# The isomorphism round's inverse deviation: Heron steps on VectorE in place of ScalarE's square root

## The chip, the cores and the metric

The kernel runs on one core of one Trainium2 chip. The metric is the device time of one execution in microseconds. The engines are PE (TensorE), ACT (ScalarE), DVE (VectorE), POOL (GpSimd) and SP (SyncE, which here only issues DMAs). The host only lays the arrays out.

## The reference

Four graph networks run one after the other over the same 50000 nodes of 128 numbers and 25000 edges. Each is followed by a residual sum and a layer norm. The change is in the second network alone, a graph isomorphism layer (GIN):

```python
def _layernorm(x, axis=-1, eps=1e-05):
    m = jnp.mean(x, axis=axis, keepdims=True)
    v = jnp.var(x, axis=axis, keepdims=True)
    return (x - m) / jnp.sqrt(v + eps)
...
        edge_emb = edge_attr @ bond_W + bond_b
...
        message = jax.nn.gelu(x[src] + edge_emb, approximate=False) * edge_weight
        agg = jax.ops.segment_sum(message, dst, num_segments=x.shape[0])
        h = (1.0 + eps) * x + agg
        h = jax.nn.relu(h @ W1 + b1)
        return h @ W2 + b2
...
    x = _layernorm(x + _L1_gnn_ref(x, edge_index, edge_attr_16, edge_weight1, L1_gnn_bond_W, L1_gnn_bond_b, L1_gnn_eps, L1_gnn_W1, L1_gnn_b1, L1_gnn_W2, L1_gnn_b2), axis=-1)
```

So every row of 128 numbers needs its mean and one divided by the root of its variance.

## The kernel before

The work is eight rounds: three of SAGE, one of GIN, two of GCN, two of RGCN. A round goes through the nodes in 49 pairs of halves; a pair is 1024 nodes, 8 blocks of 128 rows. The GIN round is the branch `k == 3` everywhere, and it takes about 1500 to 2400 us of the profile.

Each engine has its own instruction stream, written out by hand, that walks through the same steps `it` of 49 pairs; semaphores hold the streams together. No scheduler reorders anything, so each engine does its work in the order of its step function, and the pipeline between pairs comes from the offsets (`it - 1`, `it + 1`) in those functions. In most steps there is also an edge batch (896 edges, 28 of them in all), which must be ready before the next half can be summed. The order of the work within a GIN step is:

- ACT, if there is a batch: copies the weighed edge messages to half precision (L791) and forms the gelu of the next batch (L785). Then for the pair: `sums_out(it, 1)` (L831), `hidden(it, 0)` (L840), `deviation(it - 1)` (L866, the square root), `sums_out(it + 1, 0)`, four blocks of `normalise(it - 1)` (L881), `hidden(it, 1)`, the other four blocks.
- DVE, if there is a batch: the low part of the messages (L1532) and the next batch's embedding sum (L1504). Then the one-hots that turn edges into sums (L1550), `add(it - 1, 1)` (L1630), `statistics(it - 1, 1)` (L1640, L1645), `scale_rows(it - 2)` (L1757), the one-hots of the next pair's second half, `scale_and_move(it - 1)` (L1654 and L1656: inverse deviation, and minus mean times it), `add(it, 0)`, `statistics(it, 0)`.
- PE, if there is a batch: its embedding (L1075). Then per half the products of messages and one-hots (L1116, L1118), the node's own rows (L1142), the first dense layer (L1180) and the second (L1188, L1192).
- POOL weighs the messages after the gelu (L710) and issues the gathers of later batches (L680). SP loads rows and stores the normalised ones.

ACT holds one table of functions at a time. Copy, Relu and Identity stand in any table; Gelu and Sqrt stand in different ones. Loads of tables (ACT_TABLE_LOAD) are put into the stream by the compiler ahead of the instruction whose line they carry.

`wait_apart` is a wait that is an instruction of its own, followed by an increment of an unused semaphore; `wait` is carried by the instruction behind it:

```python
            eng.wait_ge(semaphore, value)
            eng.sem_inc(passed, 1)
```

Of the kernel before, what the change touches and what calls it, by code (L numbers as in the profile page):

```python
# [7 lines left out]
I32 = mybir.dt.int32  # L8
U16 = mybir.dt.uint16
ALU = mybir.AluOpType  # L10
# [27 lines left out]
GROUPS = -(-TILES // GROUP)  # L38
TURNS = BATCHES // RING
EPS = 1e-5  # L40
assert TILES % BATCH == 0 and BATCHES % RING == 0 and TILES % 2 == 0

SAGE, GIN, GCN, RGCN = "sage", "gin", "gcn", "rgcn"
# [17 lines left out]
class StepSemaphores:  # L61
# [3 lines left out]
    NAMES = ("taken", "high", "low", "every", "out", "feature", "rows", "rows_copied", "turned", "turn_copied", "agg",  # L65
             "bn", "var", "std", "rstd", "moved", "normed", "copied", "turned_edges", "masked_done", "masked_used",
             "hidden_made", "hidden_done", "scaled", "emb_done", "emb_used", "gelu_done", "weighed_edges",
             "gain_step", "gained", "bn2", "var2", "std2", "rstd2", "moved2", "normed2", "sum_made")


    def __init__(self, shared, totals, part, rel):
# [34 lines left out]
        self.weighed = one("weighed_edges", BATCHES + 1, gin)  # L106
        self.res_loaded = pair("residual", 16 * NPAIR, last and part != 4)
        self.bn_done = one("bn", NHALF, last)
        self.var_done = one("var", NPAIR, last)
        self.std_done = one("std", NPAIR, last)  # L110
        self.rstd_done = one("rstd", NPAIR, last)
        self.moved = one("moved", NPAIR, last)
        self.normed = one("normed", NPAIR, last)
# [32 lines left out]
def build_gnn(nc, A, out_ap, rounds=ROUNDS):  # L146
# [3 lines left out]
    with ctx:  # L150
        def sb(name, shape, dt=F32):
            return ctx.enter_context(nc.sbuf_tensor(name, shape, dt))
# [46 lines left out]
        mv = [sb(f"mv{n}", [P, BLOCKS, 2]) for n in range(2)]  # L199
        std = [sb(f"std{n}", [P, BLOCKS]) for n in range(2)]  # L200
        eps_col = sb("eps_col", [P, 1])
        rstd = [sb(f"rstd{n}", [P, BLOCKS]) for n in range(2)]
        nmr = [sb(f"nmr{n}", [P, BLOCKS]) for n in range(2)]
        deg = sb("deg", [P, NHALF * 4])
# [570 lines left out]
        def _(act):  # L775
# [4 lines left out]
            def sage(r, k, rel):  # L780
# [161 lines left out]
                def step(it):  # L942
# [18 lines left out]
                    if k == 0:  # L961
                        turn_copy(it, 1)
                        feature_out(it, 0)
                        table_out(it - 1, 1)
                        turn_copy(it + 1, 0)
                        feature_out(it, 1)
                        table_out(it, 0)
                    elif k == 1:
                        feature_out(it, 1)
                        table_out(it, 0)  # L970
                        feature_out(it + 1, 0)
                        table_out(it, 1)
                    elif k == 3:
                        sums_out(it, 1)
                        hidden(it, 0)
                        deviation(it - 1)
                        sums_out(it + 1, 0)
                        normalise(it - 1, (0,))
                        hidden(it, 1)
                        normalise(it - 1, (1,))  # L980
                    else:
                        feature_out(it, 1)
                        deviation(it - 1)
                        feature_out(it + 1, 0)
                        normalise(it - 1)
# [340 lines left out]
        def _(dve):  # L1326
# [170 lines left out]
            def sage_round(r, k, rel):  # L1497
# [150 lines left out]
                def scale_and_move(it):  # L1648

                    if k < 2 or not exists(it):  # L1650
# [6 lines left out]
                                           scalar=-1.0, in1=rstd[0][:, :], op0=ALU.mult, op1=ALU.mult  # L1657
                                           ).then_inc(q.moved.semaphore, 1)

                def scaled_sums(it, a):  # L1660

                    if not exists(it):
                        return
                    wait(dve, q.out_done, it * 2 + (a + 1))
                    wait(dve, q.dinv_loaded[a], it * 16 + 16)
                    wait(dve, q.rows_done, it * 2 + (a - 1))
                    V.tensor_tensor(agg_t[:, a, :], p_agg[:, a, :], dinv_row[:, a, :], ALU.mult  # L1667
                                    ).then_inc(q.feature_done.semaphore, 1)
# [92 lines left out]
                def gin_step(it):  # L1761
# [2 lines left out]
                        onehots(it + 1, now)  # L1764
                    add(it - 1, 1)
                    statistics(it - 1, 1)
                    scale_rows(it - 2)
                    if now:
                        first_onehots(it + 1, 1, after)
                    scale_and_move(it - 1)  # L1770
                    add(it, 0)
                    statistics(it, 0)

# [158 lines left out]
```

## Time and profile before

| | |
|---|---|
| median of 3 runs | 5391.27 us (5378.65 to 5395.21) |
| profiled execution, first to last instruction | 5394.1 us |
| GIN round in it, about | 1500 to 2400 us |
| mean granted TensorE clock | 0.941 |
| table loads on ACT, whole program | 150, of 1283 ns each |

The profiled execution's span lies 2.8 us above the median and 1.1 us below the longest of the three runs. In rows of groups, "busy" is the time that the engine worked on them, "mean ns" the duration of one, and "idle before" the time that the engine stood still just ahead of them, with what it was waiting for behind "<-". In rows of the timeline the idle time stands in brackets.

### The profile page before, as it was taken

Reading aid. Unit: us, or ns where it says so; the run is one execution under the profiler, and the core shown is the slowest. Engines: PE = TensorE matmul, PEld = TensorE weight load, DVE = VectorE, ACT = ScalarE, POOL = GpSimd, SP = SyncE. Lnnn points to the kernel's source line nnn. Section 1 sums busy time; section 2 is a strip of 40 time slices with the busy share of each in tenths; the row PEclk is TensorE's granted clock in tenths of the full one; section 3 lists DMA queues with packets and bytes.
Section 4 is the critical chain, followed back from the end, with each engine's and each line's share of the span. In section 5 each row is a group of like instructions: output and inputs, shape, how many; then the busy total and the mean of one; then the engine's idle time right before and its main releaser. Section 6 shows DMA issues by size and latency. Waiting matters only on the chain.

```text
span 5394.1 us, 129622 instructions
## 1 busy us (share of the span) xinstructions
PE 4403.8 (82%) x25128; PEld 2883.3 (53%) x25129; DVE 3418.7 (63%) x10510; ACT 2417.1 (45%) x4969; POOL 1920.8 (36%) x1886
## 2 busy tenths in 40 slices
PE   6998997767878888867777588887799996888895
PEld 4664554333445555435554355544577773667772
DVE  5553454676545555448997688876466663777774
ACT  2442442554357777626664466664222221333332
POOL 5650782654033433116550434310433312333310
PEclk9999999898889999989999899998899999999998
DMA  4663884555334444326563466653444433444332
GB/s 142 217 210 116 267 270 142 182 182 176 99 117 148 146 151 145 113 88 174 174 172 105 143 203 212 203 177 108 145 136 136 136 120 103 133 122 133 116 111 76
DMA packets 443919, 815.61 MB, mean 151 GB/s; under 512 B 70872, under 2 KB 76818, under 8 KB 443828
## 3 DMA queue, kind: packets, MB, share of 16 engines
q1 hardware_dynamic: 389172, 697.28, 38.6%
q0 software_dynamic: 54656, 117.32, 9.1%
q8 instruction: 33, 0.54, 0.0%
q14 instruction: 58, 0.48, 0.0%
HBM read 480.10 MB, written 334.22 MB: 151 GB/s over the span
## 4 chain that ended last, share of the span: by engine, by line
PE 46%; issue 14%; DVE 12%; ACT 8%; DVEq 6%; POOL 5%; DMA 4%; ACTq 3%; SPq 1%; POOLq 0%
PE p_agg L1116 7%; PE p_edge L1103 7%; PE p_agg L1118 6%; PE p_tr L1103 6%; PE p_agg L1149 5%; POOL raw L680 4%; DVE onehot L1550 4%; DMA h_in<-feature 3%; DVE stats L1640 3%; ACT o L881 2%; ACT u L900 2%; PE p_wide L1236 2%; PE p_agg L1142 2%; PE p_dense L1192 2%; PE p_dense L1168 2%
## 5 line engine op out<-in xcount | busy, mean ns | idle before, releaser
L1550 DVE TENSOR_SCALAR onehot<-iota,dst_f,negbase 128x512 f16<-128x512 f16 (+1 forms) x2848 | 1110.7, 444 | 823.8 <-PE p_agg L1149 304.8
L1116 PE MATMUL p_agg<-onehot,msg 128*128 128x512 f16 (+1 forms) x2848 | 1135.9, 399 | 584.9 <-DVE onehot L1550 325.1
L680 POOL DMA_INDIRECT raw<-node_s,src_i x980 | 958.1, 978 | 1462.8 <-DMA node_s<-o 560.6
L1118 PE MATMUL p_agg<-onehot,msg 128*128 128x512 f16 (+1 forms) x2848 | 1135.7, 399 | 0.0
L1116 PEld LDWEIGHTS p_agg<-onehot,msg 128*128 x2848 | 281.7, 99 | 930.7 <-issue 780.8
L680 POOL DMA_INDIRECT raw<-node_x,src_i x392 | 378.2, 965 | 553.3 <-DMA feature<-more_masked 253.7
L1149 PE MATMUL p_agg<-h_in,w 128*128 128x512 f32 x784 | 442.5, 648 | 110.6 <-DMA h_in<-feature 109.4
L881 ACT ACTIVATE o<-v_ring,nmr,rstd 128x128 f32 (+1 forms) x1176 | 472.3, 483 | 60.0 <-DVE nmr L1656 55.3
L1640 DVE BATCH_NORM_STATS2 stats<-v_ring 128x6 f32 (+1 forms) x1960 | 417.5, 278 | 44.1 <-DVE v_ring L1630 14.7
L900 ACT ACTIVATE u<-v_ring,nmr,rstd 128x128 f32 (+1 forms) x784 | 312.4, 481 | 223.9 <-DVE res_in L1686 135.6
L1118 PEld LDWEIGHTS p_agg<-onehot,msg 128*128 x2848 | 282.9, 99 | 218.9 <-issue 33.1
L851 ACT ACTIVATE u<-p_agg,bias 128x512 f32<-128x512 f32 x196 | 134.7, 687 | 551.0 <-PE p_agg L1149 550.0
L1515 DVE SCALAR_TENSOR_TENSOR hid<-type_in,p_wide 128x512 f32<-128x512 f32 (+2 forms) x456 | 261.6, 618 | 92.5 <-PE p_wide L1094 31.8
L736 POOL COPY edge_v<-raw 128x896 f32<-128x896 f32 x56 | 52.1, 930 | 705.3 <-PE p_wide L1094 693.4
L1515 DVE SCALAR_TENSOR_TENSOR more_masked<-type_in,p_wide 128x512 f32<-128x512 f32 (+2 forms) x456 | 267.0, 619 | 38.7 <-PE p_edge L1103 38.6
L851 ACT ACTIVATE u<-p_agg,sage_bias 128x512 f32<-128x512 f32 x196 | 133.8, 683 | 349.3 <-PE p_agg L1149 344.9
L866 ACT ACTIVATE std<-mv,eps_col 128x8 f32<-128x8 f32 x245 | 73.0, 298 | 453.5 <-DVE mv L1645 451.2
L1630 DVE TENSOR_TENSOR v_ring<-p_dense,res_in 128x512 f32 (+1 forms) x196 | 135.4, 691 | 208.4 <-PE p_dense L1192 173.2
L1236 PEld LDWEIGHTS p_wide<-w,u 128*128 128x128 f32 x1568 | 205.4, 192 | 99.8 <-issue 89.8
L1149 PEld LDWEIGHTS p_agg<-h_in,w 128*128 128x128 f32 x784 | 136.2, 197 | 215.9 <-DMA h_in<-feature 138.4
L1142 PEld LDWEIGHTS p_agg<-hid,h_in 128*128 128x128 f32 x1568 | 225.2, 213 | 46.6 <-issue 39.1
L1204 PE MATMUL p_dense<-w,agg_t 128*128 128x128 f32 x1568 | 234.4, 294 | 1.1 <-DVE agg_t L1667 1.1
(260 smaller groups left out, 7817.8 us busy)
## 6 DMA issues: line engine op xcount, KB each, us to landing
node_s<-o SPq DMA_DIRECT2D x392, 256.0 KB
h_in<-feature SPq DMA_DIRECT2D x392, 256.0 KB
feature<-u SPq DMA_DIRECT2D x294, 256.0 KB
node_x<-o SPq DMA_DIRECT2D x294, 256.0 KB
res_in<-node_x SPq DMA_DIRECT2D x294, 256.0 KB
h_in<-node_s SPq DMA_DIRECT2D x196, 256.0 KB
h_t<-dinv_scratch SPq DMA_DIRECT2D x196, 256.0 KB, 3.6
h_in<-in_x SPq DMA_DIRECT2D x98, 256.0 KB
```

The lines of the kernel that those rows point to most:

```text
L680: nc.gpsimd.indirect_dma_start(out=raw[:, (e % RING) * BATCH + j, :], out_offset=None, in_=src_d, in_offset=bass.IndirectOffsetOnAxis(ap=s ...
L881: last = nc.scalar.activation(o[:, b, :], tile_ap(v_ring, (it % 2) * BLOCKS + b), ACT.Identity, bias=nmr[0][:, b:b + 1], scale=rstd[0][:, ...
L900: last = nc.scalar.activation(u[:, b, :], tile_ap(v_ring, (it % 2) * BLOCKS + b), ACT.Identity, bias=nmr[0][:, b:b + 1], scale=rstd[0][:, ...
L1103: last = nc.tensor.matmul(related[part][:, j * D:(j + 1) * D], masked[m][:, j * P:(j + 1) * P], w[:, m, :], start=m == 0 and j == 0, stop= ...
L1116: nc.tensor.matmul(p_agg[:, a, :], tile_ap(msg, t, 0, D), oh, start=first, stop=True, skip_group_check=True)
L1118: return nc.tensor.matmul(p_agg[:, a, :], tile_ap(msg, t, D, 2 * D), oh, start=False, stop=True, skip_group_check=True)
L1142: last = nc.tensor.matmul(p_agg[:, a, b * P:(b + 1) * P], h_in[:, 4 * a + b, :], scaled_ident if k == 3 else two_ident, start=False, stop= ...
L1149: nc.tensor.matmul(p_agg[:, a, :], w[:, REL if rel else 3 if k == 1 else 5, :], half_buf(h_in, a), start=False, stop=True, skip_group_chec ...
L1236: last = nc.tensor.matmul(p_wide[:, a, b * D:(b + 1) * D], u[:, 4 * a + b, :], w[:, 2 if k == 0 else 4, :], start=True, stop=True)
L1515: V.scalar_tensor_tensor(out=masked[m][:, cols], in0=flat(type_in[:, bass.ds(e % RING, 1), j0 * P:j1 * P]), scalar=float(m), in1=p_wide[:, ...
L1550: return V.tensor_scalar(tile_ap(onehot, slot), iota[:, :], dst_f[:, bass.ds(t, 1)], negbase[:, bass.ds(it * 2 + a, 1)], ALU.subtract, ALU ...
L1640: last = V.bn_stats(stats[0][:, b, :], tile_ap(v_ring, (it % 2) * BLOCKS + b))
```

## The change

In the GIN round ACT no longer takes the square root of the variance. DVE forms the deviation by itself on 128x8 tiles: it divides variance plus epsilon by 16, takes half of the number's bits plus a constant as a first guess of the root, and does two Heron steps (inverse of the guess, quotient, sum) with factors chosen so that the last sum is the deviation. The inverse of that and the mean's shift follow as before. The first two operations stand ahead of `scale_rows`, the six of the Heron steps behind it, and the last two behind the one-hots, where `scale_and_move` stood. All eight new ones wait with `wait_apart` for the one ahead. The other rounds keep `deviation` and `scale_and_move`.

```diff
+HALF_BITS = float(0x1fbd1df5)
+ROOT_STEPS = 8
...
+        self.root = one("root", ROOT_STEPS * NPAIR, gin)
...
-        self.std_done = one("std", NPAIR, last)
+        self.std_done = one("std", NPAIR, last and not gin)
...
+        root_r = sb("root_r", [P, BLOCKS])
...
                         sums_out(it, 1)
                         hidden(it, 0)
-                        deviation(it - 1)
                         sums_out(it + 1, 0)
                         normalise(it - 1, (0,))
...
+                x16, guess, second = std[0], std[1], rstd[1]
+                quotient, inverse = nmr[1], root_r
+
+                def root_variance(it):
+
+                    if exists(it):
+                        wait_apart(dve, q.var_done, it + 1)
+                        V.tensor_scalar(x16[:, :], mv[0][:, :, 1:2].rearrange("p b o -> p (b o)"), EPS, 1.0 / 16.0,
+                                        ALU.add, ALU.mult).then_inc(q.root.semaphore, 1)
+
+                def root_guess(it):
+                    if exists(it):
+                        wait_apart(dve, q.root, it * ROOT_STEPS + 1)
+                        V.tensor_scalar(guess[:, :].bitcast(I32), x16[:, :].bitcast(I32), 0.5, HALF_BITS,
+                                        ALU.mult, ALU.add).then_inc(q.root.semaphore, 1)
+
+                def root_inverse(it, m):
+                    if exists(it):
+                        wait_apart(dve, q.root, it * ROOT_STEPS + m)
+                        V.reciprocal(inverse[:, :], (guess if m == 2 else second)[:, :]).then_inc(q.root.semaphore, 1)
+
+                def root_quotient(it, m):
+                    if exists(it):
+                        wait_apart(dve, q.root, it * ROOT_STEPS + m)
+                        V.scalar_tensor_tensor(out=quotient[:, :], in0=x16[:, :], scalar=1.0 if m == 3 else 4.0,
+                                               in1=inverse[:, :], op0=ALU.mult, op1=ALU.mult
+                                               ).then_inc(q.root.semaphore, 1)
+
+                def root_sum(it, m):
+                    if exists(it):
+                        wait_apart(dve, q.root, it * ROOT_STEPS + m)
+                        V.tensor_tensor((second if m == 4 else guess)[:, :], quotient[:, :],
+                                        (guess if m == 4 else second)[:, :], ALU.add).then_inc(q.root.semaphore, 1)
+
+                def inverse_and_move(it):
+                    if exists(it):
+                        wait(dve, q.normed, it)
+                        wait_apart(dve, q.root, it * ROOT_STEPS + 8)
+                        V.reciprocal(rstd[0][:, :], guess[:, :]).then_inc(q.rstd_done.semaphore, 1)
...
                     statistics(it - 1, 1)
+                    root_variance(it - 1)
+                    root_guess(it - 1)
                     scale_rows(it - 2)
+                    root_inverse(it - 1, 2)
+                    root_quotient(it - 1, 3)
+                    root_sum(it - 1, 4)
+                    root_inverse(it - 1, 5)
+                    root_quotient(it - 1, 6)
+                    root_sum(it - 1, 7)
                     if now:
                         first_onehots(it + 1, 1, after)
-                    scale_and_move(it - 1)
+                    inverse_and_move(it - 1)
                     add(it, 0)
```

On DVE, in the step of the GIN round that stands just ahead of its loop, the order before runs from the variance (`mv`) over `scale_rows` and the one-hots to the inverse deviation, which waits for ACT's `std`. What an instruction waits for stands in brackets.

```order
L1645 BN_AGGR mv<-stats 128x2 x7
L1757 TENSOR_TENSOR u<-o,dinv 128x1024 [waits normed]
...
L1550 TENSOR_SCALAR onehot<-iota,dst_f,negbase 128x512
L1654 RECIPROCAL rstd<-std 128x8 [waits normed,std]
L1656 SCALAR_TENSOR_TENSOR nmr<-mv,rstd 128x8 [waits rstd]
```

At the same place of the changed program (its lines have other numbers) the tiles `std`, `nmr`, `rstd` and `root_r` hold the steps of the root.

```order
L1648 BN_AGGR mv<-stats 128x2 x7
L1670 TENSOR_SCALAR std<-mv 128x8 [waits var]
L1676 TENSOR_SCALAR std<-std 128x8 [waits root]
L1804 TENSOR_TENSOR u<-o,dinv 128x1024 [waits normed]
L1682 RECIPROCAL root_r<-std 128x8 [waits root]
L1687 SCALAR_TENSOR_TENSOR nmr<-std,root_r 128x8 [waits root]
L1694 TENSOR_TENSOR rstd<-nmr,std 128x8 [waits root]
...
L1694 TENSOR_TENSOR std<-nmr,rstd 128x8 [waits root]
...
L1701 RECIPROCAL rstd<-std 128x8 [waits normed,root]
L1703 SCALAR_TENSOR_TENSOR nmr<-mv,rstd 128x8 [waits rstd]
```

Two operations moved in ahead of `scale_rows` and six behind it, and the wait for `std` became one for DVE's own semaphore `root`.

On ACT, in the loop of the GIN round, a step before began with the batch, each of its two activations behind a table load, and two more loads stood ahead of the pair's first copy and ahead of the root.

```order
L791 ACT_TABLE_LOAD
L791 ACTIVATE msg<-edge_v 128x7x128
L403 ISA
L785 ACT_TABLE_LOAD
L785 ACTIVATE edge_v<-edge_v 128x896
...
L831 ACT_TABLE_LOAD
L831 ACTIVATE agg_t<-p_agg 128x512
...
L866 ACT_TABLE_LOAD
L866 ACTIVATE std<-mv,eps_col 128x8
```

The same loop of the changed program has none of the four.

```order
L795 ACTIVATE msg<-edge_v 128x7x128
L407 ISA
L789 ACTIVATE edge_v<-edge_v 128x896
...
L835 ACTIVATE agg_t<-p_agg 128x512
```

The root and the four loads left the loop; one load stays ahead of the round's first gelu, and one moves to the first root of the GCN round behind it. PE, POOL and SP have the same rows as before.

## Rows read from the trace of the kernel before

**Rows 1.** The page, busy time of each engine, its share and instruction count.

```profile
PE 4403.8 (82%) x25128; PEld 2883.3 (53%) x25129; DVE 3418.7 (63%) x10510; ACT 2417.1 (45%) x4969; POOL 1920.8 (36%) x1886
```

**Rows 2.** Windows view, 36 regular steps: busy PE, PEld, DVE, ACT, POOL, PEclk, DMA.

```profile
1614.00:2211.40 597.40, 512.19 (x2630) 321.78 (x2628) 327.67 (x1050) 446.91 (x709) 207.98 (x207) 0.99 0.45 146
```

**Rows 3.** Groups on ACT, 1500 to 2400 us: busy, mean ns, idle before.

```profile
L866 ACT ACT_TABLE_LOAD x47 | 60.3, 1283 | 0.8
...
L831 ACT ACT_TABLE_LOAD x46 | 59.0, 1283 | 37.0 <-PE p_agg L1142 35.4
...
L785 ACT ACT_TABLE_LOAD x28 | 35.9, 1283 | 111.0 <-DVE edge_v L1504 111.0
...
L791 ACT ACT_TABLE_LOAD x27 | 34.6, 1283 | 0.5
```

**Rows 4.** Waits, 1600 to 2200 us: us in total, times, longest.

```profile
DVE rstd L1654 <- ACT std L866: 20.3, 24, 0.9
...
PE p_wide L1180 <- ACT hid L840: 14.9, 17, 0.9
...
PE p_agg L1142 <- DMA h_in<-node_x: 0.6, 3, 0.2
...
ACT L785 <- DVE edge_v L1504: 82.7, 24, 3.5
```

**Rows 5.** Timeline of one step with a batch: start, length, work, idle before it.

```profile
2049.72 1.28 ACT L791 ACT_TABLE_LOAD   x1
...
2051.01 0.95 ACT L791 ACTIVATE msg<-edge_v 128x896 f32 x1
...
2057.72 1.68 POOL L710 TENSOR_TENSOR edge_v<-edge_v,ew 128x896 f32<-128x896 f32 x1 [20.83 <-ACT edge_v L785]
...
2058.24 0.64 DVE L1645 BATCH_NORM_AGGREGATE mv<-stats 128x2 f32<-128x6 f32 x8 [0.15 <-DVE stats L1640]
...
2058.83 1.65 DVE L1757 TENSOR_TENSOR u<-o,dinv 128x1024 f32<-128x1024 f32 x1
...
2060.18 1.98 PE L1180 MATMUL p_wide<-agg_t,w 128*128 128x512 f32 x4 [0.85 <-ACT hid L840]
...
2062.35 0.20 DVE L1654 RECIPROCAL rstd<-std 128x8 f32<-128x8 f32 x1 [0.89 <-ACT std L866]
...
2063.19 1.65 ACT L881 ACTIVATE o<-v_ring,nmr,rstd 128x128 f32 x4 [0.39 <-DVE nmr L1656]
```

**Rows 6.** Timeline of a step without a batch, same columns.

```profile
2042.42 1.23 DVE L1757 TENSOR_TENSOR u<-o,dinv 128x1024 f32<-128x1024 f32 x1
...
2043.56 1.05 DVE L1550 TENSOR_SCALAR onehot<-iota,dst_f,negbase 128x512 f16<-128x512 f16 x3
...
2044.53 0.20 DVE L1654 RECIPROCAL rstd<-std 128x8 f32<-128x8 f32 x1
```

**Rows 7.** Groups on DVE, 1500 to 2400 us: short operations, mean ns.

```profile
L1654 DVE RECIPROCAL rstd<-std 128x8 f32<-128x8 f32 x49 | 9.8, 200 | 22.0 <-ACT std L866 22.0
...
L1656 DVE SCALAR_TENSOR_TENSOR nmr<-mv,rstd 128x8 f32<-128x8 f32 x49 | 8.2, 167 | 1.7
...
L1854 DVE TENSOR_SCALAR one_eps<-one_eps 128x1 f32<-128x1 f32 x1 | 0.2, 154 | 0.0
```

**Rows 8.** Timeline, late steps: the next add after the moved mean.

```profile
2240.60 0.69 DVE L1630 TENSOR_TENSOR v_ring<-p_dense,res_in 128x512 f32 x1 [2.16 <-PE p_dense L1192]
```

**Rows 9.** Timeline, last pair: TensorE waits for ACT's hidden rows.

```profile
2384.00 3.57 PE L1192 MATMUL p_dense<-w,hid 128*128 128x128 f32 x16 [2.62 <-ACT hid L840]
```

**Rows 10.** Timeline: TensorE waits for one-hots, in two steps.

```profile
1957.40 0.39 PE L1116 MATMUL p_agg<-onehot,msg 128*128 128x512 f16 x1 [1.69 <-DVE onehot L1550]
...
2007.15 0.39 PE L1116 MATMUL p_agg<-onehot,msg 128*128 128x512 f16 x1 [2.24 <-DVE onehot L1550]
```

**Rows 11.** Windows view behind these two waits, columns as in rows 2.

```profile
1957.40:1960.80 3.40, 2.51 (x15) 1.76 (x16) 3.10 (x14) 3.37 (x5) 2.31 (x3) 1.00 0.32 77
...
2008.60:2012.00 3.40, 3.40 (x11) 2.41 (x10) 3.07 (x12) 3.37 (x5) 2.79 (x4) 0.54 0.32 112
```

More of the change, by code:

```diff
@@ L67 @@
              "hidden_made", "hidden_done", "scaled", "emb_done", "emb_used", "gelu_done", "weighed_edges",
-             "gain_step", "gained", "bn2", "var2", "std2", "rstd2", "moved2", "normed2", "sum_made")
+             "gain_step", "gained", "root", "bn2", "var2", "std2", "rstd2", "moved2", "normed2", "sum_made")
     def __init__(self, shared, totals, part, rel):
@@ new lines, in inverse_and_move @@
+                def inverse_and_move(it):
[3 more added lines that the diff above has]
+                        V.reciprocal(rstd[0][:, :], guess[:, :]).then_inc(q.rstd_done.semaphore, 1)
+                        wait(dve, q.rstd_done, it + 1)
+                        V.scalar_tensor_tensor(out=nmr[0][:, :], in0=mv[0][:, :, 0:1].rearrange("p b o -> p (b o)"),
+                                               scalar=-1.0, in1=rstd[0][:, :], op0=ALU.mult, op1=ALU.mult
+                                               ).then_inc(q.moved.semaphore, 1)
```

## The prediction

> **What bounds the kernel now.** The page first: PE is busy for 82% of the span, DVE for 63%, ACT for 45% [rows 1]. These are averages over eight rounds, and the change touches one, so the stretch of the GIN round comes next. Its regular part, 1614.0 to 2211.4 us, is 36 steps that repeat in groups of three: a first step with an edge batch, a second with a batch, a third without. A group takes 597.4 / 12 = 49.8 us, of which PE is busy for 512.2 / 12 = 42.7, ACT for 37.2 and DVE for 27.3 [rows 2]. None of the three is full, so it is waits that set the pace, and the question is which wait ends last.
>
> ACT's groups show what is special here: 148 table loads of 1283 ns, 190 us in this round alone [rows 3]. But ACT also stands still: 3.5 us in every batch step until DVE has summed the next batch's edges [rows 4]. So a load that is taken away may only make ACT wait longer. The timeline of a batch step shows the circle [rows 5]: ACT loads a table and copies the messages (2051.01), DVE takes these over, goes through its step to the variance `mv` (2058.24 + 0.64 = 2058.88), to `scale_rows` (L1757) and the one-hots, waits 0.89 for ACT's root, forms the inverse (2062.35), ACT normalises (2063.19), and straight behind that loads the table and copies the next batch. In the second and third step together the circle runs through PE once: DVE's `add` waits for PE's rows, and from `mv` on the way is the same. In the circle, then, stand: everything on DVE from `mv` to the inverse, ACT's normalisation, and one load (L791) per batch. The other loads stand on ACT while it would wait anyhow, with one exception: in a batch step PE waits 0.85 for ACT's `hidden` [rows 4, 5].
>
> **The change part by part, per step.**
>
> *Loads.* 46 + 47 + 27 + 27 loads leave the round (one gelu load stays, one load moves to the next round's first root, where ACT waits for `mv` as it does here). Off ACT that is 147 x 1.283 = 189 us. On the circle it is L791's 1.28 alone. L831's load waits for PE's sums for 35.4 us in all [rows 3], in the steps without a batch; what PE takes from there it takes half a step later, so I count nothing for those. The Trainium skill ("ScalarE: Activation LUTs", section "What ACT_TABLE_LOAD costs") says that a load costs 1283 ns and a drain of about 1380 besides. The trace has the copy 1.29 after the load's start [rows 5], so the drain is not in this circle and gets no chance below; with it the 26 circles with a batch would give back another 26 x 1.38 = 36 us, and the time would be 5366.
>
> *The wait for the root.* In a batch step DVE's wait of 0.89 goes, and the inverse can start where it does when `std` is there early: in the third step at 2044.53, 0.08 before the one-hots' end at 2044.61 [rows 6]. So 0.97.
>
> *The eight operations.* Inverse 0.200 and quotient 0.167 are in the trace at this size; for the two scalar operations and the two sums the nearest row is a 128x1 scalar operation of 0.154 [rows 7]. Together 2 x 0.200 + 2 x 0.167 + 4 x 0.154 = 1.35 us. Each waits by `wait_apart` for the one ahead on its own engine. That handover is in the trace: `mv` behind the statistics, 0.15 [rows 5]. Of the eight, seven are in the circle with it (the first Heron operation's wait is over during `scale_rows`): 7 x 0.15 = 1.05. The lower bound is the pair L1654 and L1656, whose wait is carried by the instruction: 49 waits stood open for 1.7 us, 0.03 each [rows 7]. The upper is the 0.39 that ACT stands idle behind DVE's `nmr` [rows 5], a handover between engines with the same construct; at 0.39 the sum would be 57 us more, which I hold for under 2 in 100. I take 0.15: the same construct, on the same engine, in the same step. Further, `scale_rows` starts 0.05 before `mv` ends [rows 5], a head start that a 0.15 us operation ahead of it hardly leaves room for; the one-hots behind the last sum likewise: 0.05 twice. Sum: 1.35 + 1.05 + 0.10 = 2.50 us, on DVE's way from `mv` to the inverse, in every step.
>
> *POOL's collision.* `scale_rows` takes 1.65 in a batch step and 1.23 without [rows 5, 6]. It overlaps POOL's weighing, 2057.72 to 2059.40. The gelu loses its load, so the weighing ends 1.28 earlier, at about 2058.1, before `scale_rows` starts at 2059.4. That gives 0.42. Lower bound nothing, if POOL's gathers behind it collide too.
>
> *PE.* With the gelu's load and L831's gone, ACT's `hidden` comes 2.57 earlier and PE's wait of 0.85 vanishes. In a batch step that is not on the circle, but the third step's `add` waits for PE, so it comes 0.85 sooner.
>
> SP's stores wait for the normalised rows, and its next loads of `h_in` queue behind them; PE waited 0.6 us in all for `h_in` over 600 us [rows 4], so a shift of a microsecond costs nothing.
>
> The sum per turn: from the first batch step to the second, +2.50 - 0.97 - 0.42 - 1.28 = -0.17. From the second through the third to the next first, +2.50 - 0.85 - 1.28 = +0.37. Over the round: 12 x (-0.17) = -2.0; 13 x 0.37 = +4.8 (the irregular start has one more such turn); one early step without the other gains, +2.50 - 1.28 = +1.2. After the last batch there are six steps in which the circle is DVE's: the inverse there was ready 2.16 before the next `add` could start [rows 8], so 2.50 - 2.16, about 0.35 each, +2.1. At the end the last two pairs wait in turn for the normalisation: PE stands still for ACT's `hidden`, which queues behind it [rows 9]: 2 x 2.50 = +5.0. Total -2.0 + 4.8 + 1.2 + 2.1 + 5.0 = **+11 us**. The profiled execution would go from 5394.1 to 5405; its span is 2.8 above the median of the runs, so I set the forecast from that median: 5391.3 + 11 = **5402 us**. About 0.3% (16 us) is what a measurement of this kernel can tell from no change.
>
> So 189 us of loads leave, and the time hardly moves: what waited for ACT now waits for DVE's chain.
>
> **The rivals.**
>
> *The clock (slower).* PE's wait for one-hots in batch steps was 1.69 to 2.24. After the longer one the next 3.4 us ran at a granted clock of 0.54, close to the 1.2 GHz level; after the shorter one at 1.00 [rows 10, 11]. PE comes 0.85 earlier, so these waits grow to about 2.5 and more. In a first step a slow stretch is absorbed by slack in the second. If it falls in the second, it delays the third step's `add` by half of 3.4, 1.7 us: 12 x 1.7 = +20, so 5422. Against it: a delay in the first step eats the second's wait.
>
> *Cheap handovers (faster).* If the sequencer gets each wait out of the way while the operation ahead runs, a handover costs the carried wait's 0.03 [rows 7] instead of 0.15. Seven of them save 0.84 a turn, over 12 + 13 + 1 + 2 = 28 turns 24 us, plus 2 in the late steps, where no more than the 0.35 can be had back: 5402 - 26 = 5376. It turns faster by more than 0.3% if the operations are a little shorter than I took them, too. For it: one engine, tiny tiles. Against it: the 0.15 in this very step [rows 5]. The Trainium skill ("VectorE: DVE Perf Modes", section "The DRAIN you can't avoid") goes further and says that a semaphore behind each operation cost nothing extra; at zero it would be 5369. The two rows, 0.03 and 0.15, do not bear that out.
>
> *ACT was the bound after all (faster).* If its ten loads in a group (12.8 us) were all on a circle that I have misread, PE's 42.7 would set the group: 12 x (49.8 - 42.7) = -85, so 5306. It decides if DVE's Heron steps hide behind another wait. Against it stands ACT's idle 3.5 in each batch step.
>
> *POOL still collides (slower).* If `scale_rows` meets the gathers, the 0.42 stays in 27 batch steps: +11, so 5413.
>
> **How the numbers follow.** The even trade has 0.55, with a range of its own of 5388 to 5416, of which 0.10 lies above 5407 (bound of 0.3%); the clock 0.15; cheap handovers 0.15, of which I put 0.12 beyond -0.3%; POOL 0.10; ACT 0.05. Faster is 0.12 + 0.05 = 0.17, slower 0.10 + 0.15 + 0.10 = 0.35, same the remaining 0.48. The range leaves out ACT's case and about half each of the clock's and the cheap handovers' cases, whose times lie at its edges: 5370 to 5424.
>
> **What would show it.** In the trace afterwards: one table load in the round, ACT busy for about 24 of 50 us; ACT idle for over 3 us ahead of four normalised blocks in a batch step, released by DVE's `nmr`; the eight operations 0.3 us apart; `scale_rows` at 1.23 throughout; groups of 49.5 to 50.5 us; no PE wait for `hidden`. I would be wrong if the operations stood closer than 0.25 apart or further than 0.4, if PE's slow stretches moved into second steps, or if groups fell below 49.

## The result, and the profile after

The changed kernel takes 5431.5 us (median of 4 runs, 5427.7 to 5446.1) against 5390.1 of the kernel before on the same chip. The ratio is 1.0086, with a 95% interval of 1.0071 to 1.0101, which is 38 to 54 us. The medians differ by 41 us, where +11 with a range up to 5424 was forecast. Its profiled execution spans 5425.9 us.

The page's busy times first, then the windows view of the regular stretch (columns as in [rows 2]):

```profile
PE 4383.0 (81%) x25128; PEld 2871.0 (53%) x25129; DVE 3482.9 (64%) x10902; ACT 2212.3 (41%) x4774; POOL 1937.0 (36%) x1886
```

```profile
1614.00:2211.40 597.40, 497.57 (x2514) 311.55 (x2514) 354.22 (x1277) 266.73 (x528) 217.83 (x206) 0.97 0.43 140
```

ACT lost what the change promised: 205 us of its 2417 in the program [rows 1], 180 of 447 in this stretch [rows 2]. PE did less in the same time, 2514 matmuls against 2630: the round goes more slowly. The groups of the round (1500 to 2460 us) say what ACT and DVE do now:

```profile
L885 ACT ACTIVATE o<-v_ring,nmr,rstd 128x128 f32 x368 | 151.2, 484 | 209.4 <-DVE nmr L1703 209.4
...
L1553 DVE TENSOR_SCALAR onehot<-iota,dst_f,negbase 128x512 f16<-128x512 f16 x300 | 109.3, 421 | 49.1 <-issue 42.2 <-PE p_agg L1145 3.5
...
L1804 DVE TENSOR_TENSOR u<-o,dinv 128x1024 f32<-128x1024 f32 x49 | 60.0, 1225 | 19.2 <-issue 15.9 <-ACT o L885 3.4
...
L1676 DVE TENSOR_SCALAR std<-std 128x8 int32<-128x8 int32 x49 | 8.4, 172 | 7.7 <-DVE std L1670 0.9
...
L789 ACT ACT_TABLE_LOAD x1 | 1.3, 1283 | 18.0 <-DVE edge_v L1507 18.0
```

One table load is left of 148 [rows 3]. ACT now stands idle for 209 us (51 before) until DVE has the moved mean `nmr` (L1703). `scale_rows` takes 1.225 us throughout, as without POOL's collision [rows 5, 6]. In the idle times of `scale_rows` and of the one-hots stands "issue" (15.9 and 42.2 us): DVE stood still although no wait that the profile shows held it. Ahead of `scale_rows` that is new. Ahead of the one-hots, idle times of about 2 us stood before as well (15.8 us in eight between 1600 and 2200 us); new are the short ones, 0.25 each. The timeline of a batch step, from one message copy to the next:

```profile
2068.78 0.94 ACT L795 ACTIVATE msg<-edge_v 128x896 f32 x1
...
2076.03 0.64 DVE L1648 BATCH_NORM_AGGREGATE mv<-stats 128x2 f32<-128x6 f32 x8
2076.83 0.17 DVE L1670 TENSOR_SCALAR std<-mv 128x8 f32<-128x8 f32 x1 [0.16 <-DVE mv L1648]
...
2077.15 0.17 DVE L1676 TENSOR_SCALAR std<-std 128x8 int32<-128x8 int32 x1
...
2077.67 1.23 DVE L1804 TENSOR_TENSOR u<-o,dinv 128x1024 f32<-128x1024 f32 x1 [0.35 <-issue]
...
2078.81 0.20 DVE L1682 RECIPROCAL root_r<-std 128x8 f32<-128x8 f32 x1
2079.16 0.17 DVE L1687 SCALAR_TENSOR_TENSOR nmr<-std,root_r 128x8 f32<-128x8 f32 x1 [0.15 <-DVE root_r L1682]
...
2079.79 0.20 DVE L1682 RECIPROCAL root_r<-rstd 128x8 f32<-128x8 f32 x1
...
2080.45 0.17 DVE L1694 TENSOR_TENSOR std<-nmr,rstd 128x8 f32<-128x8 f32 x1
2080.88 1.06 DVE L1553 TENSOR_SCALAR onehot<-iota,dst_f,negbase 128x512 f16<-128x512 f16 x3 [0.25 <-issue]
2081.85 0.20 DVE L1701 RECIPROCAL rstd<-std 128x8 f32<-128x8 f32 x1
2082.08 0.17 DVE L1703 SCALAR_TENSOR_TENSOR nmr<-mv,rstd 128x8 f32<-128x8 f32 x1
2082.68 1.65 ACT L885 ACTIVATE o<-v_ring,nmr,rstd 128x128 f32 x4 [3.54 <-DVE nmr L1703]
...
2086.91 0.94 ACT L795 ACTIVATE msg<-edge_v 128x896 f32 x1
```

The way from the variance's end (2076.03 + 0.64 = 2076.67) to the moved mean's end (2082.08 + 0.17 = 2082.25) is 5.58 us. Before, in a step whose root was there early, the way was 2.47: `scale_rows` starts about 0.05 before the variance's end [rows 5], so that lies at 2042.46; the inverse starts at 2044.53 [rows 6], the moved mean 0.23 behind it, and that ends at 2044.93. So the change put +3.11 on this way, not +2.50.

Two more distances are used below, from the moved mean's start to the next copy and from the second copy of a group to the third step's `add`. Before and after, behind the copies of [rows 5] and of the timeline above:

```profile
2062.59 0.17 DVE L1656 SCALAR_TENSOR_TENSOR nmr<-mv,rstd 128x8 f32<-128x8 f32 x1
...
2068.83 0.95 ACT L791 ACTIVATE msg<-edge_v 128x896 f32 x1
...
2089.80 0.69 DVE L1630 TENSOR_TENSOR v_ring<-p_dense,res_in 128x512 f32 x1 [2.34 <-PE p_dense L1192]
```

```profile
2107.72 0.69 DVE L1633 TENSOR_TENSOR v_ring<-p_dense,res_in 128x512 f32 x1 [2.18 <-PE p_dense L1195]
```

The first went from 6.24 (2062.59 to 2068.83) to 4.83 (2082.08 to 2086.91), the second from 20.97 here, 20.90 in the median of the round, to 20.81 (2086.91 to 2107.72).

Turns, from one message copy to the next (medians; 13 and 12 of each kind, where the forecast counted 12 and 13):

| turn | before | after | forecast |
|---|---|---|---|
| first to second batch | 17.82 | 18.13 (+0.31) | -0.17 |
| second batch, through the step without, to the next first | 31.94 | 33.55 (+1.61) | +0.37 |

From the round's first moved mean to that of the next round the profiled executions took 884.3 us before and 927.4 after, +43. The two kinds of turn give 6.1 and 22.3 of it, the round's start 1.7, the late steps and the end 13.0. The rest of the program differs by 11 us the other way between these two executions; the stretch behind the round differs by as much among all profiled executions here (2949 to 2961 us).

### The profile page after: what moved, and what is told of

Same layout as the page of the kernel before. It is cut to its first block, busy times and chain, and to the rows that moved or that the text cites. A ratio compares the mean times of both kernels' runs of the same rounds, so it can differ in the third digit from the quotient of the medians.

```text
span 5425.9 us, 130708 instructions
## 1 busy us (share of the span) xinstructions
PE 4383.0 (81%) x25128; PEld 2871.0 (53%) x25129; DVE 3482.9 (64%) x10902; ACT 2212.3 (41%) x4774; POOL 1937.0 (36%) x1886
## 4 chain that ended last, share of the span: by engine, by line
PE 42%; issue 16%; DVE 15%; DVEq 7%; ACT 7%; POOL 5%; DMA 5%; ACTq 3%; SPq 1%; POOLq 0%
PE p_edge L1106 7%; PE p_agg L1119 7%; PE p_agg L1121 6%; PE p_tr L1106 5%; PE p_agg L1152 5%; POOL raw L684 4%; DVE onehot L1553 3%; DMA h_in<-feature 3%; DVE stats L1643 3%; ACT o L885 3%; ACT u L904 2%; PE p_wide L1239 2%; DVE mv L1648 2%; DVEq L1553 2%; PE p_dense L1171 2%
## 5 line engine op out<-in xcount | busy, mean ns | idle before, releaser
L1119 PE MATMUL p_agg<-onehot,msg 128*128 128x512 f16 (+1 forms) x2848 | 1132.5, 398 | 631.2 <-DVE onehot L1553 364.8
L1119 PEld LDWEIGHTS p_agg<-onehot,msg 128*128 x2848 | 281.7, 99 | 976.8 <-issue 827.6
L684 POOL DMA_INDIRECT raw<-node_x,src_i x392 | 390.8, 997 | 549.9 <-DMA feature<-more_masked 253.0
L684 POOL DMA_INDIRECT raw<-in_x,src_i x196 | 194.1, 990 | 106.5 <-issue 54.0
L1145 PE MATMUL p_agg<-hid,h_in 128*128 128x128 f32 x1568 | 231.2, 295 | 0.0
```

What stands on the lines that cost most here:

```text
L684: nc.gpsimd.indirect_dma_start(out=raw[:, (e % RING) * BATCH + j, :], out_offset=None, in_=src_d, in_offset=bass.IndirectOffsetOnAxis(ap=s ...
L1119: nc.tensor.matmul(p_agg[:, a, :], tile_ap(msg, t, 0, D), oh, start=first, stop=True, skip_group_check=True)
L1145: last = nc.tensor.matmul(p_agg[:, a, b * P:(b + 1) * P], h_in[:, 4 * a + b, :], scaled_ident if k == 3 else two_ident, start=False, stop= ...
```

## The experiments

Three theories stood at the start. **Theory 1**: DVE's way from variance to moved mean sets the pace, and was sized too small. **Theory 2**: TensorE lost the time, by its waits and a lower clock. **Theory 3**: ACT's order, with `hidden` queued behind a longer wait. All ratios are to the kernel before in the same session. Its median was 5387.7 to 5395.7 us over the sessions, so a difference in us between runs of different sessions is uncertain by some 8 us.

**The eight operations taken out.** The normalisation then uses the inverse of the variance, so the root is left out.

```diff
-                    root_variance(it - 1)
-                    root_guess(it - 1)
...
-                    root_inverse(it - 1, 2)
...
-                    root_sum(it - 1, 7)
```

> This kernel is the changed one with the eight root operations taken out; the inverse is taken of the variance itself, so the root is left out. Theory 1 (the way on DVE from the variance to the moved mean sets the pace; 5.57 us in the changed kernel against 2.47 before): the way is 2.47 again and ACT's table loads stay away, so the first-to-second batch turn falls from 18.13 to about 15.1 us, second-to-first from 33.55 to about 29.7, a group of three steps from 51.7 to 44.8, and the time to 5431 - 12 x 6.9 - about 25 in the irregular steps = about 5325 us. Theory 2 (TensorE: its longer waits bring the lower clock, or its work is next in line): a group does not fall below 48, the time stays above 5370. Theory 3 (ACT's new order, with hidden rows queued behind a longer wait, costs the time): PE still waits for ACT and the gain is under 20 us.

5336.7 us, 0.9898 [0.9881, 0.9914]: 95 below the changed kernel. Regular turns of 15.0 to 16.1 and 29.7 to 30.1; Theory 1 had 15.1, 29.7 and 5325. The time stands in these operations and what they bring with them.

**The eight operations added to the kernel before**, beside ACT's root and with all loads kept; their result is not used.

```diff
                     statistics(it - 1, 1)
+                    root_variance(it - 1)
+                    root_guess(it - 1)
                     scale_rows(it - 2)
+                    root_inverse(it - 1, 2)
...
+                    root_sum(it - 1, 7)
```

> The kernel before with ACT's root and all its table loads kept, and the eight root operations done on DVE besides, on tiles of their own, at the places where the change has them; their result is not used. Theory 1: the way from the variance to the moved mean is 5.6 us as in the changed kernel while the load ahead of ACT's copy stays on the circle; first-to-second turn 17.83 + 3.1 - 0.97 - 0.42 = 19.5 us, second-to-first 32.0 + 3.0 = 35.0, group 54.5 against 49.8, time 5390 + 12 x 4.7 + about 20 = about 5466 us. Theory 2 (the loss comes from the loads' going, by way of TensorE's waits and clock): close to before, 5390 to 5410. Theory 3 (ACT's new order): close to before as well.

5484.2, 1.0171 [1.0154, 1.0188]: 93 above the kernel before, 18 more than Theory 1 had, with turns of 19.75 and 35.4 to 36.0. The operations cost the same 93 to 95 us on either side, so the root's and the loads' absence gives back 53 us, no more, of what left ACT.

**Waits carried by the operations** in place of instructions of their own:

```diff
-                        wait_apart(dve, q.root, it * ROOT_STEPS + m)
+                        wait(dve, q.root, it * ROOT_STEPS + m)
```

> The changed kernel with the waits of the root operations carried by the operations, not standing as instructions of their own. Theory 1: seven handovers fall from 0.15 to 0.03 us, 0.84 us a turn, in 28 to 34 turns 24 to 29 us, so 5403 to 5407; if the sequencer's preparation behind short operations (0.35 idle ahead of the scaled rows, 0.26 ahead of the one-hots) shrinks too, as far as 5390. Theories 2 and 3: within 8 us of the changed kernel's 5431.

5403.1, 1.0015 [1.0003, 1.0028]: 28 us less than the changed kernel. Timeline of its Heron steps on DVE:

```profile
2011.06 1.23 DVE L1804 TENSOR_TENSOR u<-o,dinv 128x1024 f32<-128x1024 f32 x1 [0.23 <-issue]
...
2012.20 0.20 DVE L1682 RECIPROCAL root_r<-std 128x8 f32<-128x8 f32 x1
2012.43 0.17 DVE L1687 SCALAR_TENSOR_TENSOR nmr<-std,root_r 128x8 f32<-128x8 f32 x1
2012.63 0.17 DVE L1694 TENSOR_TENSOR rstd<-nmr,std 128x8 f32<-128x8 f32 x1
...
2013.27 0.17 DVE L1694 TENSOR_TENSOR std<-nmr,rstd 128x8 f32<-128x8 f32 x1
2013.79 1.06 DVE L1553 TENSOR_SCALAR onehot<-iota,dst_f,negbase 128x512 f16<-128x512 f16 x3 [0.35 <-issue]
```

A handover is 0.03 (2012.43 + 0.17 to 2012.63), not 0.15. The "issue" ahead of `scale_rows` falls from 0.35 to 0.23, and the one ahead of the one-hots is still there, 0.35.

**One Heron step less**, and so a coarser root (the first factor is 1/4 in place of 1/16):

```diff
...
-                    root_inverse(it - 1, 5)
-                    root_quotient(it - 1, 6)
-                    root_sum(it - 1, 7)
...
```

> The changed kernel with one Heron step in place of two (three operations fewer; the root is coarser). Theory 1: the way on DVE is shorter by 0.20 + 0.167 + 0.167 + 3 x 0.15 = 0.98 us in each of 28 to 34 turns, so 27 to 33 us less, 5398 to 5404; a turn from batch to batch falls from 18.13 to 17.15. Theory 2: under 10 us, since TensorE's waits for one-hots stay over 2.2 us in the first steps. Theory 3: under 10 us.

5400.2, 1.0011 [1.0001, 1.0021]: 31 us less, and the batch turn is 17.15, 0.98 shorter: the distance from the first Heron operation to the fourth in the changed kernel (2078.81 to 2079.79). These four fit Theory 1, within 18 us, and not the other two.

**What queues behind DVE's way.** Three runs move one line each, or both: the one-hots ahead of the six Heron operations (DVE), and `hidden` of the second half ahead of the first four normalised blocks (ACT).

```diff
+                    if now:
+                        first_onehots(it + 1, 1, after)
                     root_inverse(it - 1, 2)
...
-                    if now:
-                        first_onehots(it + 1, 1, after)
```

```diff
                         sums_out(it + 1, 0)
+                        hidden(it, 1)
                         normalise(it - 1, (0,))
-                        hidden(it, 1)
                         normalise(it - 1, (1,))
```

> The changed kernel with one line moved on VectorE: the one-hots of the next pair's second half stand ahead of the six Heron operations (behind scale_rows) and not behind them. Theory 1 (VectorE's way from the variance to the moved mean alone makes the time): that way stays within 0.2 us of the changed kernel's 5.57 (0.35 of preparation ahead of the one-hots goes, a handover of 0.15 ahead of the inverse comes), so at most 28 x 0.2 = 6 us faster, 5426 to 5432. Theory 1 with what is queued behind that way (the one-hots stand behind the Heron operations, TensorE waits 1.32 us for them, and the step without a batch pays): besides those 6 us, 0.6 to 1.0 us less in each of 13 turns through TensorE, 8 to 13 us, so 5412 to 5419, and TensorE's wait for one-hots of 1.3 us in the second batch step is gone.

> The changed kernel with one line moved on ScalarE: hidden of the second half stands ahead of the first four normalised blocks and not behind them, so it no longer queues behind their wait for VectorE's moved mean. Theory 1 (VectorE's way alone): the turn from first to second batch stays at 18.13. What queues behind the way: TensorE's wait for hidden of 0.33 us in the turn through the step without a batch goes, 33.55 to 33.2, 13 x 0.33 = 4 us; its wait for the one-hots behind the Heron operations (1.32) stays. In the last two pairs TensorE no longer waits for hidden behind the normalisation, 2 x 2.5 to 3.3 = 6 us. Together about 5421 (5415 to 5429).

> Both lines moved: on VectorE the one-hots ahead of the six Heron operations, on ScalarE hidden ahead of the normalised blocks. With the one-hots alone moved the turn through the step without a batch fell only from 33.55 to 33.33, since TensorE then waited 0.30 us for hidden. If the two waits behind the way together ate the gain on TensorE that the prediction counted (0.85), this turn falls below both single moves, to 32.9 (32.7 to 33.05), and the time to 5413 (5406 to 5422). If something else ate it, the turn stays at 33.2 or above, and only the last two pairs gain, 5421.

One-hots alone: 5429.9, 1.0073 [1.0057, 1.0089], nothing that the time can tell from the changed kernel. The turns fell by 0.11 and 0.22, where the queue was expected to give 0.6 to 1.0 in each turn through TensorE. `hidden` alone: 5396.2, 1.0013 [1.0001, 1.0025], far below what was expected. Both: 5385.3, 0.9995 [0.9982, 1.0008], below that too. The stretches of a turn (medians from the timelines; in the first row of `hidden` the values of two kinds of turn) say why:

| us | changed | one-hots | hidden | both |
|---|---|---|---|---|
| second copy to the third step's `add` | 20.81 | 20.70 | 20.41; 20.67 to 20.89 | 20.07 |
| moved mean's start to the next copy | 4.83 | 4.84 | 3.69 | 3.70 |

The first row is TensorE's part. The one-hots alone take off 0.11. `hidden` alone takes off 0.40 in the four turns whose first batch step ran at a granted clock of 1.00; in seven others it fell to 0.50 in that step, the second step's own `add` came 0.3 to 0.4 later, and little of the gain is left. Both together take off 0.74, more than the sum. The second row was missed by every theory: `hidden` of the second half stands between the two normalisations, ahead of the next copy, and so on the circle itself, in the kernel before too. Moving it takes 1.14 off each turn, 25 times 1.14 = 29 us of the 35, and another 5 at the last pair (13.81 to 8.56). It is no part of the 41 us, since it stood there before.

The timeline of the changed kernel shows both waits in the turn through the step without a batch:

```profile
2100.55 0.39 PE L1119 MATMUL p_agg<-onehot,msg 128*128 128x512 f16 x1 [1.33 <-DVE onehot L1553]
...
2100.82 1.65 ACT L885 ACTIVATE o<-v_ring,nmr,rstd 128x128 f32 x4 [4.89 <-DVE nmr L1703]
...
2102.37 1.24 ACT L844 ACTIVATE hid<-p_wide,b_col 128x512 f32<-128x512 f32 x2
...
2103.09 0.30 PEld L1183 LDWEIGHTS p_wide<-agg_t,w 128*128 128x128 f32 x2 [0.34 <-ACT hid L844]
```

With both lines moved, the same place of that kernel:

```profile
2025.02 0.69 ACT L844 ACTIVATE hid<-p_wide,b_col 128x512 f32<-128x512 f32 x1 [0.17 <-PE p_wide L1183]
...
2028.25 0.39 PE L1119 MATMUL p_agg<-onehot,msg 128*128 128x512 f16 x1 [0.97 <-issue]
...
2028.73 3.19 ACT L885 ACTIVATE o<-v_ring,nmr,rstd 128x128 f32 x8 [3.02 <-DVE nmr L1703]
...
2030.51 1.88 PE L1183 MATMUL p_wide<-agg_t,w 128*128 128x512 f32 x4
```

In the changed kernel `hidden` starts 1.55 us behind the normalisation; with both moved even its second part starts 3.7 ahead of it (2025.02 against 2028.73). TensorE has a wait for neither left there. It still stands idle for 0.97 us ahead of L1119 with no wait shown (0.7 at this place in the kernel before).

**The Heron steps in one piece**: `scale_rows` ahead of the add, the one-hots behind the moved mean. The same with carried waits, and with `hidden` ahead besides.

```diff
+                    scale_rows(it - 2)
                     add(it - 1, 1)
...
-                    scale_rows(it - 2)
...
+                    inverse_and_move(it - 1)
                     if now:
                         first_onehots(it + 1, 1, after)
-                    inverse_and_move(it - 1)
```

> The changed kernel with scale_rows moved ahead of the add, and the one-hots moved behind the moved mean: the ten operations from the variance to the moved mean then stand in one piece on VectorE, and no other work lies between them. Theory 1 (that way sets the pace): the way from the variance's end to the moved mean's end falls from 5.57 us to 1.8 of operations and 10 x 0.15 of handovers, 3.3 us. Turn from first to second batch: scale_rows still lies on it, ahead of the add, so 18.13 - 1.1 = 17.0; turn through TensorE: scale_rows lies where VectorE waits for TensorE, so 33.55 - 2.3 = 31.2. A group 48.2 against 51.7: 12 x 3.5 = 42 us, with the starts and the late steps some 60 us: 5370 (5355 to 5390). Were ScalarE's order or TensorE the bound, the time would stay within 10 us of 5431.

> As the run in one piece, and the eight waits of the Heron steps carried by the operations behind them, in place of wait instructions of their own. Theory 1: eight handovers fall from 0.15 to 0.03 us, about 1.0 us a turn over 28 turns, 27 us below the run in one piece, so about 5343 (5330 to 5360), unless TensorE, whose waits were already short at 5337 without the eight operations, begins to limit the turns.

> The fastest kernel so far (the Heron operations in one piece, their waits carried, 5328 us) with hidden ahead of the normalised blocks. Theory 1: the turn from first to second batch, which ends on VectorE's way, stays at 15.78. The turn through TensorE may lose its waits for hidden, up to 0.3 us each, and the last two pairs up to 6 us: 5318 (5310 to 5330).

In one piece: 5370.9, 0.9957 [0.9940, 0.9974], turns 16.84 and 31.1. With carried waits: 5328.3, 0.9883 [0.9861, 0.9905], turns 15.78 and 29.14; 43 us rather than 27 came off, since the turn through TensorE fell by 1.97, not by 1.0 (its `add` came 0.9 earlier). With `hidden` ahead: 5307.8, 0.9852 [0.9833, 0.9871], turns 14.9 and 28.2. The last expectation's unmoved 15.78 is wrong for the reason above. DVE in that kernel:

```profile
2036.53 0.64 DVE L1648 BATCH_NORM_AGGREGATE mv<-stats 128x2 f32<-128x6 f32 x8 [0.15 <-DVE stats L1643]
...
2037.21 0.17 DVE L1670 TENSOR_SCALAR std<-mv 128x8 f32<-128x8 f32 x1
...
2039.14 0.17 DVE L1703 SCALAR_TENSOR_TENSOR nmr<-mv,rstd 128x8 f32<-128x8 f32 x1
...
2039.66 0.74 DVE L1553 TENSOR_SCALAR onehot<-iota,dst_f,negbase 128x512 f16<-128x512 f16 x2 [0.36 <-issue]
```

The way is 2.14 us (2037.17 to 2039.31) in place of 5.58. Its "issue" of 0.36 now falls behind the moved mean, off the way.

**The better orders without the change**: the kernel before with `scale_rows` ahead of the add, and with `hidden` ahead besides.

> The kernel before, with ScalarE's root and its loads, and scale_rows moved ahead of the add, as in the run in one piece: what that order is worth without the change. Theory 1: from first to second batch the root on ScalarE ends last and not VectorE's work, so that turn stays at 17.8; through TensorE the inverse may come up to 0.4 us earlier, until it waits for the root (a load of 1.28 and the root behind the variance): 13 x 0.4 = 5 us. So 5384 to 5392. If the order alone were worth what the run in one piece shows, this would be near 5340.

> The kernel before, with ScalarE's root, and both reorderings that paid: scale_rows ahead of the add (alone 5374) and hidden of the second half ahead of the normalised blocks. It asks what the change is worth where both sides have the better order, against 5308 with the Heron steps. Theory 1: on ScalarE the root already ends at the point where hidden's input is ready, so in the batch turn the normalisation moves back by about 0.9 us and the next copy comes forward by 1.1, 17.83 to 17.6; through the step without a batch, where ScalarE waits for the moved mean, the whole 1.1, 30.74 to 29.6. 12 x 1.4 us, and 5 at the end: 5353 (5345 to 5365). Were the root's removal worth nothing in itself, this would come out near 5308.

The first: 5373.7, 0.9970 [0.9958, 0.9983]; the batch turn stays at 17.84, the turn through TensorE falls by 1.2, not 0.4. The expectation put ACT's load behind the variance; the timeline has the root alone there, the load lies in the wait ahead of it:

```profile
1832.46 1.28 ACT L866 ACT_TABLE_LOAD   x1
...
1835.53 0.64 DVE L1645 BATCH_NORM_AGGREGATE mv<-stats 128x2 f32<-128x6 f32 x8 [0.15 <-DVE stats L1640]
...
1836.21 0.30 ACT L866 ACTIVATE std<-mv,eps_col 128x8 f32<-128x8 f32 x1 [2.46 <-DVE mv L1645]
```

The second: 5358.0, 0.9942 [0.9920, 0.9963], as expected. So with a better order on both sides the Heron steps are worth about 50 us (5307.8 against 5358.0; 49 by the ratios), where as written they cost 41. The two orders are not the same: the one-hots behind the moved mean were tried with the Heron steps alone, so part of the 50 may be theirs.

## Why the prediction was wrong

**The mechanism held.** That the loads hide behind ACT's waits, that one of them per batch is on the circle, and that DVE's chain takes the place of what ACT did, is what the traces show. One load is left, ACT is busy for 23 us of a group of 51.7, idle for 3.5 us ahead of the normalised blocks, the operations start 0.31 to 0.35 apart, `scale_rows` is at 1.23 and the wait for the root is gone. A group takes 51.7 us, not 49.5 to 50.5, and TensorE does wait for `hidden`, in the turn through the step without a batch. The loss that the profile gives per regular turn follows from the same terms with two of them corrected.

**Step that failed: the cost of the eight operations, 2.50 us.** It measured 3.11. The handovers were right (0.15, 0.16), the operations slightly short (0.172 and 0.167 for the 0.154 taken). The mis-sized term is the lost head starts, "0.05 twice". From the second short operation's end to `scale_rows` 0.35 passes, where the head start of 0.05 is lost besides, and 0.25 from the last sum to the one-hots: 0.65 for the 0.10 taken. The sizes add 0.06, and 2.50 + 0.55 + 0.06 = 3.11. With the corrected way and ACT's part shorter by 1.41 instead of 1.28 (moved mean to copy, 6.24 before, 4.83 after), the first turn is 3.11 - 0.97 - 0.42 - 1.41 = +0.31, as measured.

**Step that failed: "PE's wait of 0.85 vanishes, so the third step's add comes 0.85 sooner."** The wait did vanish in the batch step, but the `add` came only 0.09 sooner (20.90 to 20.81). TensorE's next work waits for the one-hots (1.33) and for `hidden` (0.34), and both queue behind DVE's longer way, one on DVE and one on ACT. The runs show that each holds gain back while the other is out of the way: 0.11 comes with the one-hots moved, 0.40 at most with `hidden`, 0.74 with both. With this term the second turn is 3.11 - 0.09 - 1.41 = +1.61, as measured.

**The late steps** were forecast at +0.35 each, as 2.50 less the 2.16 of spare time [rows 8]. With 3.11 it is +0.95; they measured +1.1 to +2.7. The mechanism was right, the spare time was used up. Of three equal steps, two measured +1.1 at a mean granted clock of 0.92, as before, and one +2.2 at 0.85; what the other three lose beyond the +0.95 is open. The last two pairs, forecast at +2.50 each, measured +0.1 and +3.3.

**The rivals.** *The clock*: TensorE's waits in first batch steps did grow to 2.9 us. Behind the wait at 2074.76 the granted clock is 0.50, behind one of 1.77 at 2092.85 it is 1.00. But behind another of 2.88, at 2126.44, it stays at 1.00, so the length of the wait alone does not decide it (and the slow stretch of [rows 11] begins 1.45 us behind the end of its wait). The waits, and the windows view behind the three, columns as in [rows 2]:

```profile
2074.76 0.60 PE L1119 MATMUL p_agg<-onehot,msg 128*128 128x512 f16 x1 [2.88 <-DVE onehot L1553]
...
2126.44 0.39 PE L1119 MATMUL p_agg<-onehot,msg 128*128 128x512 f16 x1 [2.88 <-DVE onehot L1553]
```

```profile
2074.76:2077.29 2.53, 2.53 (x7) 1.14 (x7) 1.92 (x15) 1.02 (x2) 2.23 (x3) 0.50 0.40 115
2092.85:2095.05 2.20, 2.20 (x15) 1.64 (x16) 1.74 (x14) 1.06 (x2) 1.90 (x3) 1.00 0.30 87
2126.44:2128.64 2.20, 2.20 (x15) 1.65 (x16) 1.74 (x14) 1.02 (x2) 1.90 (x3) 1.00 0.25 94
```

The slow stretch falls into ten of thirteen first steps, and the turn around it takes 18.12 to 18.14 with it and without it: slack absorbs it. Twice it fell into a second step, and there the turn took 34.11 and 34.14 in place of 33.55, 0.6 us more where this rival reckoned 1.7. *Cheap handovers*: not with wait instructions, but with carried waits they came at 0.03, and saved 28 us where this rival reckoned 26. The Trainium skill ("VectorE: DVE Perf Modes", section "The DRAIN you can't avoid") has a semaphore behind each of eight copies at nothing extra; the traces have 0.03 in the one form and 0.15 in the other. (At zero the rival's own terms give 5402 - 28 x 1.05 - 2 = 5371, not 5369.) *ACT as the bound* did not occur. *POOL's collision* left `scale_rows`, but came back elsewhere. In one pair of the regular part DVE has five one-hots to form instead of three; the weighing, which now comes earlier, overlaps the fourth, and the five take 3.21 us in place of 1.82. After and before:

```profile
2177.12 3.21 DVE L1553 TENSOR_SCALAR onehot<-iota,dst_f,negbase 128x512 f16<-128x512 f16 x5
...
2178.17 1.68 POOL L714 TENSOR_TENSOR edge_v<-edge_v,ew 128x896 f32<-128x896 f32 x1 [22.39 <-ACT edge_v L789]
```

```profile
2154.96 1.82 DVE L1550 TENSOR_SCALAR onehot<-iota,dst_f,negbase 128x512 f16<-128x512 f16 x5
...
2157.30 1.68 POOL L710 TENSOR_TENSOR edge_v<-edge_v,ew 128x896 f32<-128x896 f32 x1 [20.78 <-ACT edge_v L785]
```

The batch turn there took 20.25 instead of 18.13 and the next turn 35.65 instead of 33.55, 4 of the 41 us. Before, the pair cost nothing in its batch turn (17.83).

## What to carry to other kernels

Cost a chain of short operations by the distance of their starts, with what the next long operation loses behind them, and not by their durations; then write it in one piece, with carried waits, so that other work stands ahead of it or behind it but not in it. When a wait on the circle gets longer, list what is queued behind it on every engine, since a gain elsewhere comes only when all of that is out of the way: here two moved lines gave 0.11 and at most 0.40 us alone and 0.74 together. And a change that loses in one order may win in another: the same Heron steps cost 41 us as written, and in the best order tried the kernel is 80 us faster than the kernel before, which gains some 30 to 38 of these by a better order alone.

## What was not expected of the hardware

DVE stands still for 0.22 to 0.36 us between a short 128x8 operation and a following wider one, with no wait that the profile shows; behind `scale_rows` the next starts 0.09 before its end (2078.81 against 2078.90). The trace does show what lies in that time. `DVEq` is DVE's sequencer, which is not counted as busy; these are its instructions on the lines of the one-hots and of `scale_rows`, in the step of the timeline above (count, shortest, median and longest in ns, first and last start):

```profile
L1553 DVEq ALU_OP  x2: 45/45/45, 2080.6 to 2080.6; - x2
L1553 DVEq FUSED_REGOPS  x3: 65/65/93, 2080.7 to 2081.1; - x3
...
L1804 DVEq FUSED_REGOPS  x1: 71/71/71, 2077.6 to 2077.6; - x1
```

They are register instructions of the wider operation. Ahead of the first one-hot they run from 2080.57 to 2080.81, around the short operation's end (2080.62) and up to the one-hot's start (2080.88). That the idle time is theirs, and that a longer operation ahead would cover it, fits these times but is argued: no run took them away. And the same dependence between two operations of one engine cost 0.15 us with a wait instruction of its own and 0.03 with a carried wait, in the same place of the same program.
